# A projection stage that normalises and transposes its own input

## The chip, the cores and the metric

The kernel runs on one core of one Trainium2 chip. A core has a matrix engine (TensorE, PE in the profile; PEld is its weight load), a vector engine (VectorE, DVE), a scalar engine (ScalarE, ACT), a general one (GpSimd, POOL) and a synchronisation engine (SyncE, SP) that here only issues DMAs. The queue of DMAs that SyncE issues is q1, that of ScalarE q10. Each engine runs its own instructions in their order and meets the others at semaphores. The metric is the device time of one execution in microseconds; lower is better.

## The reference

The model has two layers on 8 sequences of 1024 tokens, 256 wide, all in float32. Only its first step matters here:

```python
def _layernorm(x, axis=-1, eps=1e-05):
    m = jnp.mean(x, axis=axis, keepdims=True)
    v = jnp.var(x, axis=axis, keepdims=True)
    return (x - m) / jnp.sqrt(v + eps)
...
def proj(W, b):
    return (x @ W + b).reshape(B, T, NUM_HEADS, HEAD_DIM).transpose(0, 2, 1, 3)
q = _rope(proj(Wq, bq))
k = _rope(proj(Wk, bk))
v = proj(Wv, bv)
```

Here `x` is the layer-normalised input. `_rope` multiplies two halves of each head by cosines and sines of the position and adds or subtracts them. Softmax attention over 16 heads, an output projection with a residual, a routed expert layer, a phase-memory attention and a soft mixture of experts follow; none of them is touched.

## The kernel before

The kernel is a row of stages. Each is a `Stage` with its own SBUF and PSUM buffers; at each start GpSimd raises every semaphore of the stage by one and all engines meet at a barrier, so that nothing of a stage overlaps the one before it. What passes between stages lies in DRAM.

Stage `n0` (`normalise`, lines 84 to 226) reads the 8 sequences, 1024 rows at a time. VectorE takes the statistics (`bn_stats` L149, `bn_aggr` L154), ScalarE the square root (L199), VectorE the reciprocal and minus mean over deviation (L166, L167) and the normalised rows (L175); TensorE transposes them, 16 tiles of 128x128 per sequence (L191), ScalarE copies them out of PSUM (L217) and stores the transposed array `xnT` (L222). For this stage no untransposed normalised rows are stored. The same function also serves two later stages, `n1` and `n3`.

Stage `qkv` (`qkv_rope`, from L229) takes 512 tokens at a time, 16 blocks. SyncE loads a block of `xnT` (L269) into one of four buffers. TensorE makes 128x512 products for the queries (two, each over two halves of the width: 4 matmuls), the same for the keys, both at L311, and 8 matmuls of 256 columns for the values (L318). A float32 matmul stands in the trace as two records of MATMUL, so a block has 16 of the first kind and 16 of the second. VectorE multiplies each product by the cosines and by the sines (L332, L333: four operations per unit, a unit being the queries or the keys of a block), GpSimd subtracts and adds (L350, L351, two operations per unit), VectorE adds the bias to the values (L340), and ScalarE issues the stores (L289, L293). Each engine's order is written out by hand. The products have two PSUM buffers, the values two as well.

In the code, `FLOOR` is the one by which each semaphore was raised; `made`, `multiplied`, `turned_ready`, `v_made` and `v_ready` count units or blocks that were finished by TensorE, VectorE, GpSimd, TensorE and VectorE.

## Time and profile before

| | |
|---|---|
| Median of 3 runs | 5393.15 us (5390.27 to 5396.76) |
| Span of the profiled execution, its own time | 5387.6 us |
| TensorE busy | 4725.5 us, 88% |
| VectorE busy | 3304.6 us, 61% |
| ScalarE busy | 2124.8 us, 39% |
| GpSimd busy | 1122.3 us, 21% |
| First instruction of the `qkv` stage's TensorE | 88.97 us after the span's start |
| First DMA of the attention stage | 266.82 us |

The profile is one execution; its span runs from the first to the last instruction, and its time is given by this span alone. The median of the timed runs is 5.6 us above it: that is what lies around the span, with the spread of the runs. In timelines a row is a run of like instructions: its start, how long it lasted together, engine, line, operation, output and inputs with buffer numbers left out, shapes and count; a bracket at the end is the engine's idle time before it and what ended that.

### The profile page before, as it was taken

The numbers are of one execution on the slowest core, as the hardware profiler recorded it, in microseconds if no ns is written. First come the engines' busy times: TensorE is split into PE (matmuls) and PEld (weight loads), VectorE is DVE, ScalarE is ACT, GpSimd is POOL, SyncE is SP. The second block draws the span as 40 slices with busy tenths as digits, with TensorE's granted clock in tenths as the row PEclk, the third lists the DMA queues.
The fourth block names the chain that finished last, engine by engine and source line by source line (L and its number), as shares of the span: only waits on it lengthen the run. The fifth ranks groups of instructions, "written<-read, shape, count | busy, mean of one in ns | idle before, by whom it ended". The sixth has DMA issues, their size and how long they took to land. (4 is left out here: it accounts for less than half of the span.)

```text
span 5387.6 us, 72176 instructions
## 1 busy us (share of the span) xinstructions
PE 4725.5 (88%) x28132; PEld 3108.0 (58%) x28132; DVE 3304.6 (61%) x3937; ACT 2124.8 (39%) x3450; POOL 1122.3 (21%) x848
## 2 busy tenths in 40 slices
PE   5879999999999755599997778774999999979999
PEld 3512222222222144488886334434899999968888
DVE  5578888888888344322222687775677676644443
ACT  1037777776677501122222434332222222223332
POOL 1432112222211020244442000000233333310000
PEclk9979999999999875799998889886999999989999
DMA  6543454443444184443433101109645444455543
GB/s 215 184 68 56 62 86 78 66 78 67 76 70 70 46 309 147 130 81 81 86 79 91 59 24 47 47 26 316 136 100 99 99 99 98 97 157 181 175 177 129
DMA packets 470402, 578.35 MB, mean 107 GB/s; under 512 B 32032, under 2 KB 384672, under 8 KB 461728
## 3 DMA queue, kind: packets, MB, share of 16 engines
q1 hardware_dynamic: 262816, 399.15, 28.6%
q10 hardware_dynamic: 182784, 142.62, 11.2%
q0 software_dynamic: 24576, 33.57, 3.8%
q8 instruction: 141, 2.31, 0.2%
q14 instruction: 85, 0.70, 0.1%
HBM read 297.23 MB, written 227.67 MB: 97 GB/s over the span
## 5 line engine op out<-in xcount | busy, mean ns | idle before, releaser
L743 DVE TENSOR_REDUCE att_nmx<-att_s 128x1 f32<-128x1024 f32 x1024 | 1204.9, 1219 | 230.9 <-PE att_s L653 227.6
L729 ACT ACTIVATE att_pt<-att_sT 128x512 f32<-128x512 f32 x2048 | 1058.9, 603 | 470.2 <-PE att_sT L670 469.6
L653 PE MATMUL att_s<-att_KT,att_QT 96*128 96x512 bf16 x2048 | 790.1, 390 | 48.1 <-DMA att_KT<-att_hi 38.0
L670 PE MATMUL att_sT<-att_QT,att_KT 128*128 128x512 bf16 x2048 | 778.2, 383 | 6.1 <-ACT att_pt L729 6.1
L1895 POOL TENSOR_TENSOR sl_lg<-sl_lg,sl_sm 128x512 f32<-128x512 f32 x256 | 319.5, 1269 | 1498.6 <-DVE sl_sm L2033 1498.6
L670 PEld LDWEIGHTS att_sT<-att_QT,att_KT 128*128 128x128 bf16 x2048 | 197.6, 97 | 650.1 <-ACT att_pt L729 466.9
L684 PE MATMUL att_o<-att_pt,att_va 128*32 128x512 f32 x4096 | 553.4, 607 | 0.0
L1906 PE MATMUL sl_lp<-sl_phi,sl_xT 128*128 (+1 forms) x4160 | 491.0, 277 | 36.5 <-DMA sl_xT<-xnT 22.8
L1906 PEld LDWEIGHTS sl_lp<-sl_phi,sl_xT 128*128 128x128 f32 x4160 | 478.4, 193 | 43.5 <-issue 43.5
L2146 PE MATMUL cb_op<-cb_y,cb_exT 128*128 128x256 f32 x2048 | 485.5, 380 | 0.0
L1944 PE MATMUL sl_acc<-sl_lg,sl_xn 128*128 128x128 f32 x4096 | 478.3, 275 | 0.0
L1944 PEld LDWEIGHTS sl_acc<-sl_lg,sl_xn 128*128 128x128 f32 x4096 | 467.7, 192 | 0.0
L1966 ACT ACTIVATE sl_lg<-sl_lg 128x1024 f32<-128x1024 f32 x128 | 135.3, 1057 | 767.2 <-DVE sl_lg L2022 767.2
L1356 DVE TENSOR_TENSOR moe_hT<-moe_sg,moe_up 128x512 f32<-128x512 f32 x128 | 88.1, 688 | 532.8 <-PE moe_yp L1221 325.4
L2146 PEld LDWEIGHTS cb_op<-cb_y,cb_exT 128*128 128x128 f32 x2048 | 370.7, 191 | 40.2
L653 PEld LDWEIGHTS att_s<-att_KT,att_QT 96*128 96x128 bf16 x2048 | 198.5, 99 | 244.7 <-DVE att_nmx L743 50.1
L2031 DVE TENSOR_REDUCE sl_sm<-sl_lg 128x128 f32<-128x1024 f32 x128 | 248.6, 1942 | 136.5 <-ACT sl_lg L1966 136.5
L1154 POOL DMA_INDIRECT x<-moe_y,moe_idx x128 | 213.2, 1666 | 344.2 <-ACT moe_y L1272 324.6
L579 POOL COPY att_QT<-att_QT 32x1024 bf16<-32x1024 bf16 x64 | 72.5, 1159 | 921.1 <-DVE att_QT L764 920.9
L1207 PE MATMUL moe_gp<-moe_xT,moe_wg 128*128 128x256 f32 x1024 | 244.0, 381 | 1.7 <-DVE moe_bo L1374 0.9
L1207 PE MATMUL moe_up<-moe_xT,moe_wu 128*128 128x256 f32 x1024 | 242.4, 380 | 0.0
L1221 PE MATMUL moe_yp<-moe_wd,moe_hT 128*128 128x256 f32 x1024 | 231.6, 379 | 1.4 <-DVE moe_hT L1356 1.4
(217 smaller groups left out, 6075.3 us busy)
## 6 DMA issues: line engine op xcount, KB each, us to landing
lg<-sl_raw ACTq DMA_DIRECT2D x128, 512.0 KB, 6.0
cb_ex<-lg SPq DMA_DIRECT2D x64, 1024.0 KB, 5.9
xnT<-n_xnT ACTq DMA_DIRECT2D x48, 512.0 KB, 5.5
n_x<-x SPq DMA_DIRECT2D x18, 1024.0 KB, 10.2
sl_w<-in_L_ffn_W SPq DMA_DIRECT2D x68, 256.0 KB, 3.5
qk<-qkv_turned ACTq DMA_DIRECT2D x64, 256.0 KB, 3.2
att_qin<-qk SPq DMA_DIRECT2D x64, 256.0 KB, 9.1
xn<-n_xn ACTq DMA_DIRECT2D x16, 1024.0 KB, 9.6
```

Of the source, the lines that this page charges most:

```text
L653: ins = pe.matmul(s[i % 2][:, c, :], QT[n % NB][0:ROWS, h, t * P:(t + 1) * P], KT[n % NB][0:ROWS, h, c * 512:(c + 1) * 512], start=True, s ...
L670: pe.matmul(sT[:, idx % 3, :], KT[g % NB][:, h, kt * P:(kt + 1) * P], QT[g % NB][:, h, step // 4 * 512:(step // 4 + 1) * 512], start=True, ...
L684: ins = pe.matmul(o[32 * h:32 * h + 32, :], va[g % 2][:, kt, h, :], pt[:, step % 2, h, c, :], start=kt == 0, stop=kt == NT - 1)
L729: act.activation(pt[:, step % 2, h, c, :], sT[:, idx % 3, :], ACT.Exp, scale=HD ** -0.5).then_inc(exp_done, 1)
L743: dve.tensor_reduce(nmx[n % 2][:, t, h:h + 1], s[i % 2][:].rearrange("p c k -> p (c k)"), AX.X, ALU.max, negate=True).then_inc(freed, 1)
L1207: ins = pe.matmul(o_[:, m, :], w_[:, k, (2 * h + m) * P:(2 * h + m + 1) * P], xT[n % 2][:, k, :], start=k == 0, stop=k == KD - 1)
L1221: ins = pe.matmul(yp[n % 2][:, s, :], hT[m // 2][:, m % 2, s * P:(s + 1) * P], wd[e][:, m, :], start=m == 0, stop=m == NI - 1)
L1895: pool.tensor_tensor(part_, part_, sm[j][:].rearrange("p (a n) -> p a n", a=1).broadcast_to([P, HB, P]), ALU.mult).then_inc(shared, 1)
L1906: ins = pe.matmul(lp[j][:, b, :], xT[:, k, b * T + m * P:b * T + (m + 1) * P], ph[:, k, bass.ds(c * P, P)], start=k == 0, stop=k == KD - 1)
L1944: ins = pe.matmul(acc[:, k, b, :], xn[:, b * NT + m, k * P:(k + 1) * P], lg[m % 4][:, b, :], start=m == 0 and b % 4 == 0, stop=m == NT - 1 ...
L2031: ch.link(dve.tensor_reduce(sm[j][:], lg[l][:].rearrange("p b n -> p n b"), AX.X, ALU.add))
L2146: ins = pe.matmul(op[n % 2][:], exT[n % 2][:, s, :], y[b % 2][:, s, :], start=s == 0, stop=s == SK - 1)
```

## The change

The separate stage `n0` is gone. `qkv_rope` now loads raw rows, 512 tokens at a time, into four buffers `xr` and does for each block what `n0` did: statistics (4 tiles of 256 elements), square root, reciprocal and scaled mean on VectorE and ScalarE. The normalised rows `xn` are now made by ScalarE (four operations with scale and bias per block) instead of VectorE. TensorE transposes 8 tiles of 128x128 into one PSUM buffer `tr`, and ScalarE takes all 1024 elements per partition out at once into `xT`. `xT` has two buffers instead of four, and the PSUM buffer of the values one instead of two. All stores of the stage are issued by SyncE instead of ScalarE, in one order with the loads: queries, next block's rows, keys, values.

```diff
-def qkv_rope(nc, xnT_d, wqk_d, ...
+def qkv_rope(nc, x_d, wqk_d, bqk_d, wv_d, bv_d, cos_d, sin_d, ident_d, qk_d, v_d):
...
+        xr = [st.sb(f"xr{j}", [P, TB, D]) for j in range(NR)]
+        xn = [st.sb(f"xn{j}", [P, TB, D]) for j in range(2)]
+        xT = [st.sb(f"xT{j}", [P, KD, N]) for j in range(2)]
-        vm = [st.ps(f"vm{j}", [P, N // P, D]) for j in range(2)]
+        vm = st.ps("vm", [P, TB, D])
+        tr = st.ps("tr", [P, KD, N])
...
             def _(sp):
                 def tokens(i):
-                    if i >= NX:
-                        sp.wait_ge(v_made, FLOOR + i - NX + 1)
-                    sp.dma_start(xT[i % NX][:], xnT_d[:, :, i * N:(i + 1) * N].rearrange("k p t -> p k t")
-                                 ).then_inc(x_in[i % NX], 16)
+                    if i >= NR:
+                        sp.wait_ge(xn_ready, FLOOR + i - NR + 1)
+                    sp.dma_start(xr[i % NR][:], rows(x_d, i)).then_inc(x_in[i % NR], 16)
...
                 tokens(0)
+                sp.dma_start(ident[:], ident_d).then_inc(ident_in, 16)
+                tokens(1)
                 sp.dma_start(wqk[:], wqk_d.rearrange("(k p) c n -> p k c n", p=P)).then_inc(c_in, 16)
...
+                tokens(2)
+                tokens(3)
+                for i in range(BLOCKS):
+                    unit_out(2 * i)
+                    if i + NR < BLOCKS:
+                        tokens(i + NR)
+                    unit_out(2 * i + 1)
+                    sp.wait_ge(v_ready, FLOOR + i + 1)
+                    sp.dma_start(rows(v_d, i), v[i % NV][:]).then_inc(v_stored[i % NV], 16)
...
             @block.tensor
+                def turn(i):
+                    pe.wait_ge(xn_ready, FLOOR + i + 1)
+                    if i >= 1:
+                        pe.wait_ge(xT_ready, FLOOR + i)
+                    for k in range(KD):
+                        for t in range(TB):
+                            ins = pe.transpose(tr[:, k, t * P:(t + 1) * P], xn[i % 2][:, t, k * P:(k + 1) * P], ident[:])
+                    ins.then_inc(across, 1)
...
+                pe.wait_ge(ident_in, FLOOR + 16)
+                turn(0)
+                pe.wait_ge(c_in, FLOOR + 16 * 6)
+                for i in range(BLOCKS):
+                    pe.wait_ge(xT_ready, FLOOR + i + 1)
+                    queries_or_keys(i, 0)
+                    if i + 1 < BLOCKS:
+                        turn(i + 1)
+                    queries_or_keys(i, 1)
+                    values(i)
...
             @block.scalar
+                def normal(i):
+                    act.wait_ge(nmr_ready, FLOOR + i + 1)
+                    if i >= 2:
+                        act.wait_ge(across, FLOOR + i - 1)
+                    for t in range(TB):
+                        ins = act.activation(xn[i % 2][:, t, :], xr[i % NR][:, t, :], ACT.Identity,
+                                             bias=nmr[i % 2][:, t:t + 1], scale=rstd[i % 2][:, t:t + 1])
+                    ins.then_inc(xn_ready, 1)
+                def take_turned(i):
+                    act.wait_ge(across, FLOOR + i + 1)
+                    if i >= 2:
+                        act.wait_ge(v_made, FLOOR + i - 1)
+                    act.activation(xT[i % 2][:], tr[:], ACT.Copy).then_inc(xT_ready, 1)
...
+                deviation(0)
+                normal(0)
+                deviation(1)
+                take_turned(0)
+                normal(1)
                 for i in range(BLOCKS):
+                    if i + 1 < BLOCKS:
+                        take_turned(i + 1)
+                    if i + 2 < BLOCKS:
+                        deviation(i + 2)
+                        normal(i + 2)
...
             @block.vector
+                for i in range(BLOCKS):
+                    rotate(2 * i)
+                    if i + 2 < BLOCKS:
+                        statistics(i + 2)
+                    rotate(2 * i + 1)
+                    if i + 2 < BLOCKS:
+                        scales(i + 2)
+                    dve.wait_ge(v_made, FLOOR + i + 1)
...
-    normalise(nc, "n0", x0, None, xnT, ident)
-    qkv_rope(nc, xnT, a["wqk"], ...
+    qkv_rope(nc, x0, a["wqk"], ... ident, qk, v)
```

`rotate` holds the four multiplications of a unit as they stood; `statistics` the `bn_stats` and `bn_aggr`; `scales` the reciprocal of `rstd`, then `nmr` from `mv` and `rstd`; `deviation` the square root. All four names take the place of lines that stood in `normalise` or `qkv_rope`.

On TensorE, a block before (the first; `mm` are the products of queries and keys, `vm` the values, x4 and x8 count matmuls):

```order
L311 MATMUL qkv_mm0<-qkv_xT0,qkv_wqk 128x512 x4
L311 MATMUL qkv_mm1<-qkv_xT0,qkv_wqk 128x512 x4
L318 MATMUL qkv_vm0<-qkv_wv,qkv_xT0 128x256 x8
L311 MATMUL qkv_mm0<-qkv_xT1,qkv_wqk 128x512 x4
L311 MATMUL qkv_mm1<-qkv_xT1,qkv_wqk 128x512 x4
```

And TensorE at the same place in the changed kernel, from the stage's first instruction on (`tr` is the transposes' PSUM buffer):

```order
L333 MATMUL qkv_tr<-qkv_ident,qkv_xn0 128x128 x8
L343 MATMUL qkv_mm0<-qkv_xT0,qkv_wqk 128x512 x4
L333 MATMUL qkv_tr<-qkv_ident,qkv_xn1 128x128 x8
L343 MATMUL qkv_mm1<-qkv_xT0,qkv_wqk 128x512 x4
L353 MATMUL qkv_vm<-qkv_wv,qkv_xT0 128x256 x8
L343 MATMUL qkv_mm0<-qkv_xT1,qkv_wqk 128x512 x4
L333 MATMUL qkv_tr<-qkv_ident,qkv_xn0 128x128 x8
L343 MATMUL qkv_mm1<-qkv_xT1,qkv_wqk 128x512 x4
```

The eight transposes of the next block stand between the queries and the keys of the present one.

VectorE in the first block before:

```order
L332 SCALAR_TENSOR_TENSOR qkv_by_cos0<-qkv_mm0,qkv_bqk,qkv_cos 128x512
L333 SCALAR_TENSOR_TENSOR qkv_by_sin0<-qkv_mm0,qkv_bqk,qkv_sin 128x512
L332 SCALAR_TENSOR_TENSOR qkv_by_cos1<-qkv_mm1,qkv_bqk,qkv_cos 128x512
L333 SCALAR_TENSOR_TENSOR qkv_by_sin1<-qkv_mm1,qkv_bqk,qkv_sin 128x512
L332 SCALAR_TENSOR_TENSOR qkv_by_cos1<-qkv_mm1,qkv_bqk,qkv_cos 128x512
L333 SCALAR_TENSOR_TENSOR qkv_by_sin1<-qkv_mm1,qkv_bqk,qkv_sin 128x512
L340 TENSOR_TENSOR qkv_v0<-qkv_vm0,qkv_bv 128x1024
```

VectorE in the first block of the changed kernel, from the end of the queries' unit on (`stats0`, `mv0`, `rstd0` and `nmr0` belong to the block after next):

```order
L436 SCALAR_TENSOR_TENSOR qkv_by_cos0<-qkv_mm0,qkv_bqk,qkv_cos 128x512
L437 SCALAR_TENSOR_TENSOR qkv_by_sin0<-qkv_mm0,qkv_bqk,qkv_sin 128x512
L411 BN_STATS qkv_stats0<-qkv_xr2 128x6 x4
L415 BN_AGGR qkv_mv0<-qkv_stats0 128x2 x4
L436 SCALAR_TENSOR_TENSOR qkv_by_cos1<-qkv_mm1,qkv_bqk,qkv_cos 128x512
L437 SCALAR_TENSOR_TENSOR qkv_by_sin1<-qkv_mm1,qkv_bqk,qkv_sin 128x512
L436 SCALAR_TENSOR_TENSOR qkv_by_cos1<-qkv_mm1,qkv_bqk,qkv_cos 128x512
L437 SCALAR_TENSOR_TENSOR qkv_by_sin1<-qkv_mm1,qkv_bqk,qkv_sin 128x512
L423 RECIPROCAL qkv_rstd0<-qkv_rstd0 128x4
L425 SCALAR_TENSOR_TENSOR qkv_nmr0<-qkv_mv0,qkv_rstd0 128x4
L456 TENSOR_TENSOR qkv_v0<-qkv_vm,qkv_bv 128x1024
```

The statistics stand between the two units, the reciprocal and `nmr` right behind the second unit and ahead of the values. `nmr` reads two tensors in SBUF.

## Rows read from the trace of the kernel before

**Rows 1.** The page's head.

```profile
span 5387.6 us, 72176 instructions
```

**Rows 2.** Windows: stretch, length, busy (count) by engine, clock, DMA share, GB/s.

```profile
0.00:78.00 78.00, 31.46 (x128) 25.10 (x128) 53.04 (x225) 21.36 (x42) 0.20 (x4) 1.00 0.66 230
78.00:89.00 11.00, 0.03 (x1) 0.03 (x1) 0.00 (x0) 0.00 (x0) 0.00 (x0) 1.00 0.91 277
89.00:256.00 167.00, 166.86 (x512) 97.81 (x512) 105.74 (x144) 0.00 (x0) 78.16 (x63) 1.00 0.60 186
```

**Rows 3.** Timeline, all engines, first stage: start us, length us, engine, line, operation.

```profile
2.41 0.45 SPq L128 DMA_DIRECT2D n_x<-in_x  x1
...
8.09 2.71 DVE L149 BATCH_NORM_STATS2 n_stats<-n_x 128x6 f32<-128x256 f32 x8 [5.55 <-DMA n_x<-in_x]
10.95 0.64 DVE L154 BATCH_NORM_AGGREGATE n_mv<-n_stats 128x2 f32<-128x6 f32 x8
...
12.97 0.30 ACT L199 ACTIVATE n_rstd<-n_mv,n_eps 128x8 f32<-128x8 f32 x1
...
15.04 0.17 DVE L166 RECIPROCAL n_rstd<-n_rstd 128x8 f32<-128x8 f32 x1
...
15.58 2.67 DVE L175 TENSOR_SCALAR n_xn<-n_x,n_rstd,n_nmr 128x256 f32<-128x256 f32 x8 [0.17 <-DVE n_nmr L167]
...
18.39 1.96 PE L191 MATMUL n_tr<-n_ident,n_xn 128*128 128x128 f32 x8 [18.39 <-DVE n_xn L175]
```

**Rows 4.** Timeline, all engines, between the first two stages.

```profile
77.96 0.37 SPq L269 DMA_DIRECT2D qkv_xT<-xnT  x1
...
88.97 8.63 PE L311 MATMUL qkv_mm<-qkv_xT,qkv_wqk 128*128 128x512 f32 x16 [18.69 <-DMA qkv_bv<-in_L_attn_bv]
```

**Rows 5.** Timeline, all engines, one block of the projection stage.

```profile
100.90 7.03 PE L311 MATMUL qkv_mm<-qkv_xT,qkv_wqk 128*128 128x512 f32 x16
...
104.53 0.75 DVE L332 SCALAR_TENSOR_TENSOR qkv_by_cos<-qkv_mm,qkv_bqk,qkv_cos 128x512 f32<-128x512 f32 x1 [2.21 <-PE qkv_mm L311]
...
107.34 1.27 POOL L350 TENSOR_TENSOR qkv_turned<-qkv_by_cos,qkv_by_sin 128x512 f32<-128x512 f32 x1 [4.39 <-DVE qkv_by_sin L333]
107.76 3.62 PE L318 MATMUL qkv_vm<-qkv_wv,qkv_xT 128*128 128x256 f32 x16
...
110.77 1.27 POOL L350 TENSOR_TENSOR qkv_turned<-qkv_by_cos,qkv_by_sin 128x512 f32<-128x512 f32 x1 [0.93 <-DVE qkv_by_sin L333]
...
111.22 7.03 PE L311 MATMUL qkv_mm<-qkv_xT,qkv_wqk 128*128 128x512 f32 x16
111.42 1.23 DVE L340 TENSOR_TENSOR qkv_v<-qkv_vm,qkv_bv 128x1024 f32<-128x1024 f32 x1 [0.72 <-PE qkv_vm L318]
```

**Rows 6.** Windows: a stretch of the second normalisation.

```profile
1990.00:2030.00 40.00, 21.82 (x89) 17.44 (x90) 34.34 (x148) 13.45 (x27) 0.00 (x0) 0.50 1.01 362
```

**Rows 7.** Timeline, TensorE, the same stretch.

```profile
1999.59 1.97 PE L191 MATMUL n_tr<-n_ident,n_xn 128*128 128x128 f32 x8 [1.21 <-ACT n_xnT L217]
```

**Rows 8.** Timeline, TensorE, last stage: transposes between matmuls.

```profile
5300.48 0.60 PE L2132 MATMUL cb_tr<-cb_ident,cb_ex 128*128 128x128 f32 x4
5300.92 1.89 PE L2146 MATMUL cb_op<-cb_y,cb_exT 128*128 128x256 f32 x8
```

**Rows 9.** Timeline, GpSimd and VectorE, in the attention stage.

```profile
1274.29 4.50 POOL L599 TENSOR_TENSOR att_num<-att_num,att_rb 128x2048 f32<-128x2048 f32 x1 [31.58 <-DMA att_num<-ctxT]
...
1274.33 4.51 DVE L754 CAST att_naug<-att_nrest 128x32 bf16<-128x32 f32 x1
```

**Rows 10.** Groups by line, ScalarE: count | busy us, mean ns | idle before.

```profile
L1970 ACT ACTIVATE sl_raw<-sl_lp 128x1024 f32<-128x1024 f32 x128 | 128.8, 1006 | 0.0
```

**Rows 11.** Timeline, ScalarE, scaled 256 elements, experts stage.

```profile
2506.22 0.84 ACT L1272 ACTIVATE moe_y<-moe_yp,moe_wt 128x256 f32<-128x256 f32 x2 [2.86 <-PE moe_yp L1221]
```

**Rows 12.** DMA view, 0 to 30 us: rate in 40 equal slices.

```profile
GB/s 0 0 0 0 26 83 296 382 384 348 339 355 351 347 347 350 345 347 350 350 350 320 23 0 0 22 147 284 384 386 175 0 0 0 53 61 232 429 396 384
```

**Rows 13.** The page, DMA issues: count, KB each, us to landing.

```profile
qk<-qkv_turned ACTq DMA_DIRECT2D x64, 256.0 KB, 3.2
```

More of the change, by code:

```diff
@@ L243, in qkv_rope @@
         sin = st.sb("sin", [P, T])
-        xT = [st.sb(f"xT{j}", [P, KD, N]) for j in range(NX)]
+        eps = st.sb("eps", [P, 1])
+        xr = [st.sb(f"xr{j}", [P, TB, D]) for j in range(NR)]
+        stats = [st.sb(f"stats{j}", [P, TB, 6]) for j in range(2)]
+        mv = [st.sb(f"mv{j}", [P, TB, 2]) for j in range(2)]
+        rstd = [st.sb(f"rstd{j}", [P, TB]) for j in range(2)]
+        nmr = [st.sb(f"nmr{j}", [P, TB]) for j in range(2)]
+        xn = [st.sb(f"xn{j}", [P, TB, D]) for j in range(2)]
+        xT = [st.sb(f"xT{j}", [P, KD, N]) for j in range(2)]
         by_cos = [st.sb(f"by_cos{j}", [P, 2, N]) for j in range(2)]
@@ L260, in qkv_rope @@
         table = lambda tab, u: tab[:, u // 2 % HALVES * N:(u // 2 % HALVES + 1) * N]
+        rows = lambda d, i: d[i * N:(i + 1) * N, :].rearrange("(t p) d -> p t d", p=P)
         with st.block() as block:
@@ L278, in _ @@
                 sp.dma_start(bv[:], col_bcast(bv_d)).then_inc(c_in, 16)
-                for i in range(1, BLOCKS):
-                    tokens(i)
+                tokens(2)
[7 more added lines that the diff above has]
+                    sp.dma_start(rows(v_d, i), v[i % NV][:]).then_inc(v_stored[i % NV], 16)
@@ new lines, in _, with queries_or_keys, values @@
+                for j in range(NO):
+                    sp.wait_ge(stored[j], FLOOR + 32 * (UNITS // NO))
+                for j in range(NV):
+                    sp.wait_ge(v_stored[j], FLOOR + 16 * len(range(j, BLOCKS, NV)))
+            @block.tensor
+            def _(pe):
+                def turn(i):
[6 more added lines that the diff above has]
+                    ins.then_inc(across, 1)
+                def queries_or_keys(i, w):
+                    u = 2 * i + w
+                    if u >= 2:
+                        pe.wait_ge(multiplied, FLOOR + u - 1)
+                    for two in range(2):
+                        for k in range(KD):
+                            ins = pe.matmul(mm[w][:, two, :], wqk[:, k, 2 * w + two, :], xT[i % 2][:, k, :],
+                                            start=k == 0, stop=k == KD - 1)
+                    ins.then_inc(made, 1)
+                def values(i):
+                    if i >= 1:
+                        pe.wait_ge(v_ready, FLOOR + i)
+                    for t in range(TB):
+                        for k in range(KD):
+                            ins = pe.matmul(vm[:, t, :], xT[i % 2][:, k, t * P:(t + 1) * P], wv[:, k, :],
+                                            start=k == 0, stop=k == KD - 1)
+                    ins.then_inc(v_made, 1)
+                pe.wait_ge(ident_in, FLOOR + 16)
[8 more added lines that the diff above has]
+                    values(i)
@@ L322, in _, with statistics @@
             @block.vector
             def _(dve):
-                dve.wait_ge(c_in, FLOOR + 16 * 6)
-                for u in range(UNITS):
+                def statistics(i):
+                    dve.wait_ge(x_in[i % NR], FLOOR + 16 * (i // NR + 1))
+                    for t in range(TB):
+                        ins = dve.bn_stats(stats[i % 2][:, t, :], xr[i % NR][:, t, :])
+                    ins.then_inc(stats_ready, 1)
+                    dve.wait_ge(stats_ready, FLOOR + i + 1)
+                    for t in range(TB):
+                        ins = dve.bn_aggr(mv[i % 2][:, t, :], stats[i % 2][:, t, :])
+                    ins.then_inc(var_ready, 1)
@@ new lines, in scales @@
+                def scales(i):
+                    dve.wait_ge(dev_ready, FLOOR + i + 1)
+                    if i >= 2:
+                        dve.wait_ge(xn_ready, FLOOR + i - 1)
+                    dve.reciprocal(rstd[i % 2][:], rstd[i % 2][:]).then_inc(rstd_ready, 1)
+                    dve.wait_ge(rstd_ready, FLOOR + i + 1)
+                    dve.scalar_tensor_tensor(nmr[i % 2][:], mv[i % 2][:, :, 0], -1.0, rstd[i % 2][:], ALU.mult, ALU.mult
+                                             ).then_inc(nmr_ready, 1)
```

84 lines of the change are left out of this document (38 added, 46 removed).

## The prediction

> **What bounds the kernel now.** I read first the page's head [rows 1] and its table of slices, to see that TensorE is the busiest engine nearly everywhere but at the start and in the gaps between stages; then the windows of the first 267 us, because the page's chain of waits is followed back from the end and says nothing of the start. In the windows [rows 2] the reader should see three kinds of stretch. From 0 to 78 us, the first normalisation, TensorE is busy 31.46 of 78 us and VectorE 53.04. From 78 to 89 us no engine works at all: the barrier is passed and the projection waits for its constants. From 89 to 256 us TensorE is busy 166.86 of 167 us and VectorE only 105.74, GpSimd 78.16, ScalarE 0: the projection stage is bound by TensorE. The timeline of a block [rows 5] shows the same in small: the matmuls of queries and keys start at 100.90, those of the values at 107.76, the next block's at 111.22, without a gap, a period of 10.32 us (16 records of 0.43 and 16 of 0.215). VectorE starts a unit 0.2 us behind its four matmuls (100.90 + 8 x 0.43 = 104.33, and 104.53) and waits 2.21 us for it. So work for ScalarE is free here, work for VectorE is free up to some 4 us a block, and work for TensorE is paid in full.
>
> **The change part by part.** The sum is made against the profiled execution's span, 5387.6 us; the timed median lies 5.6 us above it, and I carry that over.
>
> What goes: everything before the first matmul at 88.97 us [rows 4]. What comes instead is a new start, and then transposes inside a stage that TensorE bounds.
>
> The new start has two paths, and the later one decides. Both begin at SyncE's first DMA, at 2.41 us before [rows 3]. The stage now raises 28 semaphores instead of the 18 of the first normalisation; those 18 and the barrier took less than 2.0 us, so ten more cost between 0 and 1.1 us. I take 0.6: first DMA at 3.0.
> - Rows path. One megabyte landed 8.09 - 2.41 = 5.7 us after its issue. Half of it, at the 350 GB/s of [rows 12], lands 1.5 us sooner: 7.2. From the start of the statistics to the end of the square root it took 8.09 to 13.27 = 5.2 us with the loading of the function table; four tiles instead of eight take off half of 2.71 and half of 0.64, so 3.5: 10.7. Reciprocal and `nmr` take 15.58 - 15.04 = 0.54: 11.3. The normalised rows are new on ScalarE; the nearest row is a scaled operation of 256 elements, two in 0.84 [rows 11], so four in 1.6: 12.9 (VectorE needed 2.67 for eight, 1.3 for four, so either end is near). Eight transposes 1.96 [rows 3] and a handover of 0.1: 15.0. One copy of 1024 elements out of PSUM, 1.0 [rows 10], with 0.2 for the handovers: 16.2.
> - Constants path. Before, from the first DMA of the stage to the first matmul took 88.97 - 77.96 = 11.0 us [rows 4]. Now the identity and a second block of rows, 0.58 MB, stand ahead of the constants, 1.7 us at 350 GB/s: 3.0 + 12.7 = 15.7.
>
> So the first matmul of queries stands at 16.2 instead of 88.97: 72.8 us saved. Bounds: 14.5 if the semaphores cost nothing and the handovers are shorter, 18.5 if the two paths disturb one another. The slow start of TensorE is paid in both kernels: its first 16 records took 8.63 instead of 7.03 [rows 4, 5].
>
> Transposes: eight a block. The row of the first stage, eight in 1.96, seems to say 0.22 each. But the same operation takes the same time, 1.97, in the second normalisation [rows 7], where the granted clock is 0.50 [rows 6], that is the level of 1.2 GHz; so I read the clock of 1.00 shown for the first 78 us as not measured, and 0.22 as the slow level's price. In the last stage, where transposes stand between float32 matmuls at 1.00 (2.4 GHz), four take 5300.92 - 5300.48 = 0.44, or 0.11 each [rows 8]. The projection stage keeps TensorE busy without a gap, so its transposes should be of that kind: 8 x 0.11 = 0.87 us a block, a period of 10.32 + 0.87 = 11.19. The first block's transposes are in the start; 15 are left: 13.1 us added. Bounds: 0.87 and 1.76 a block.
>
> What lies beside TensorE. Take as zero the end of a block's query matmuls. VectorE begins at 0.2 and hands over to GpSimd 2.81 later (104.53 to 107.34 [rows 5]): 3.0. Four `bn_stats`, a gap and four `bn_aggr` take 1.36 + 0.15 + 0.32 = 1.8: 4.8. The key matmuls were done at 0.87 + 3.43 = 4.3, so VectorE begins them 0.3 us late, at 4.8, and ends at 7.6. Reciprocal and `nmr`: 8.2. ScalarE's four: 9.9. The transposes that want these rows stand one period on, at 11.19. Slack 1.3 us, so nothing. This is the wait that the change adds on TensorE, and behind it in its order stand the keys and the values: were it late, all of them would be, and VectorE with them. VectorE's work in a block is 2 x 2.81 + 1.8 + 0.54 + 1.23 = 9.2 of 11.19, ScalarE's 1.0 + 0.3 + 1.6 = 2.9. The single PSUM buffer of the values is read by VectorE within some 1.5 us after the last value matmul, and is wanted again 3.43 + 0.87 + 3.43 us later; the single one of the transposes is copied out in 1.2 us and wanted a block later. Nothing.
>
> The two operands of `nmr`. A small VectorE operation beside a running GpSimd one can be held: a cast of 128x32 took 4.51 us and ended with GpSimd's operation of 4.50 [rows 9]. Others run beside GpSimd unhindered: the addition to the values keeps its 1.23 though GpSimd started at 110.77, and GpSimd starts each unit about 0.1 us behind VectorE's last operation [rows 5], exactly where `nmr` now stands. If `nmr` waits for one GpSimd operation of 1.27 us, it is ready at 9.1 and the rows at 10.8: slack 0.4, still nothing. I take that. The Trainium skill ("SBUF — State Buffer", section "Who interferes with whom") says that VectorE and GpSimd share a pair of ports as an exclusive lock, and that a VectorE operation with two inputs in SBUF is fully blocked by a GpSimd one that reads SBUF. By that rule `nmr` is held in each block, where without it nothing would be; the trace agrees on the blocking, with 4.51 us, and by either reading the sum stays.
>
> Queue. All 2 MB a block now go through SyncE's queue: five issues besides the load, behind waits for GpSimd and VectorE. A block's rows are asked for two blocks before their statistics, 22 us, against landing times of 3 to 8 us. At 11.19 us a block that is 187 GB/s; this queue alone gave 350 in the first 20 us [rows 12]. Nothing. The stage's end has the same operations as before, so the tail to the attention stage is unchanged.
>
> Sum: -72.8 + 13.1 = -59.7 us. Span 5327.9, timed median **5333.5 us**.
>
> **The rivals.**
> - *Held twice.* GpSimd's two operations of a unit follow one another without a gap; if `nmr` gets through only behind both, it is ready at 10.3 and the rows at 12.0, 0.8 late. The chain reaches over two blocks, so a block pays half, 0.4: 14 x 0.4 = 5.6, 5339 us. For it: nothing shows who is let in first between two GpSimd operations. Against: after the cast of [rows 9] VectorE went on at once.
> - *Transposes at the slow price.* 15 x (1.76 - 0.87) = 13.3 more, 5347 us. For it: the only rows of this operation in this form, [rows 3, 7]. Against: the clock.
> - *`bn_stats` held too.* If the statistics also wait for both GpSimd operations (2.5 us), VectorE's block is 2.81 + 2.5 + 1.8 + 2.81 + 1.5 + 1.23 with 0.2 for a wait = 12.9 us and becomes the bound: 15 x 1.7 = 26, 5359 us. No row shows `bn_stats` beside GpSimd; the unhindered addition of [rows 5] speaks against.
> - *The one queue goes one transfer at a time.* Four stores of 3.2 us [rows 13] and two transfers twice their size, at least 3.2 each: 19.2 us a block instead of 11.19, 15 x 8.0 = 120 more, 5453 us, slower than before. It decides from a period of 11.19 + 59.7/16 = 14.9 us on. Against it: [rows 12], where the transfers of that queue overlapped, else 350 GB/s could not stand beside 5.7 us for one megabyte. The Trainium skill ("DMA: Bandwidth & Descriptors", section "Issuing engines are not separate DMA queues") has the queues of SyncE and ScalarE run on the same 16 engines, which would make the move free; no run here shows it yet.
>
> **How the numbers follow.** Forecast 0.66, held twice 0.13, slow transposes 0.08, `bn_stats` held 0.07, serial queue 0.03, and 0.03 for something larger that none of these names. The range: down by the start's lower bound (1.7) and the spread of the runs (3.6), 5328; up over held twice and the slow transposes with some of the start's upper bound, 5349. About 0.13 is left out. A change within 0.2%, 10.8 us, is what a measurement of this kernel cannot tell from none. All cases but the serial queue and part of the unnamed are faster by more: faster 0.95, same 0.01, slower 0.04.
>
> **What would show it.** In the changed profile: first matmul of queries near 16 us; TensorE's block every 11.2 us, with eight transposes taking 0.9 (1.8 would be the slow price) and no wait on them; `nmr` 0.2 or 1.3 or 2.5 us long; `bn_stats` four in 1.4, not 3.9; first DMA of the attention stage near 266.8 - 59.7 = 207. The forecast is wrong if TensorE waits for the normalised rows, or if the first matmul stands beyond 20 us.

## The result and the profile after

The changed kernel takes 5324.59 us (median of 4 runs, 5319.97 to 5327.42) against 5391.71 us for the kernel before (4 runs, 5387.21 to 5396.76) on the same chip: a ratio of 0.9877, 95% interval 0.9863 to 0.9891. The forecast was 5333.5 us with a range of 5328 to 5349. The gain was larger than forecast, and the time lies 3.4 us below the range. Two repetitions later gave 5322.05 and 5323.04 us, with ratios of 0.9877 and 0.9876.

The page of the profile after begins:

```profile
span 5323.5 us, 71820 instructions
```

That answers to [rows 1], 64.1 us less. This execution's own time was 5325.72 us, so 2.2 us lie around the span.

The windows of the first 208 us, in the columns of [rows 2]:

```profile
0.00:16.30 16.30, 1.94 (x8) 1.57 (x8) 4.22 (x21) 4.95 (x9) 0.20 (x4) 1.00 0.70 244
16.30:195.00 178.70, 178.64 (x625) 109.11 (x626) 143.82 (x282) 50.43 (x89) 77.07 (x62) 1.00 0.56 169
195.00:208.00 13.00, 1.86 (x9) 1.30 (x7) 2.40 (x3) 0.09 (x1) 2.81 (x3) 0.74 0.39 121
```

The reader should see that the 89 us ahead of the first matmul have become 16.3, and that in the whole stage behind it TensorE is busy 178.64 of 178.70 us: it never waits for the rows that VectorE and ScalarE now make.

The start, timeline of all engines, in the columns of [rows 3]:

```profile
3.19 0.46 SPq L290 DMA_DIRECT2D qkv_xr<-in_x  x1
...
7.06 1.40 DVE L411 BATCH_NORM_STATS2 qkv_stats<-qkv_xr 128x6 f32<-128x256 f32 x4 [3.74 <-DMA qkv_xr<-in_x]
8.50 0.38 DVE L415 BATCH_NORM_AGGREGATE qkv_mv<-qkv_stats 128x2 f32<-128x6 f32 x4
8.96 1.28 ACT L373 ACT_TABLE_LOAD   x1 [8.96 <-DVE qkv_mv L415]
10.26 0.30 ACT L373 ACTIVATE qkv_rstd<-qkv_mv,qkv_eps 128x4 f32<-128x4 f32 x1
...
10.80 0.16 DVE L425 SCALAR_TENSOR_TENSOR qkv_nmr<-qkv_mv,qkv_rstd 128x4 f32<-128x4 f32 x1
...
13.21 1.94 PE L333 MATMUL qkv_tr<-qkv_ident,qkv_xn 128*128 128x128 f32 x8 [13.21 <-ACT qkv_xn L381]
...
16.36 5.68 PE L343 MATMUL qkv_mm<-qkv_xT,qkv_wqk 128*128 128x512 f32 x8 [1.20 <-ACT qkv_xT L390]
```

The chain is the forecast one: rows, statistics, square root behind the loading of its table, normalised rows, transposes, copy out of PSUM, first matmul at 16.36 us where 16.2 was worked out. The bracket of the last row says that it waited for the copy. The last of the constants, the values' bias, had been issued at 7.20 and landed 8.2 us later, at 15.4 (forecast for that path: 15.7), so the two paths end within a microsecond of each other.

One block, timeline of all engines, answering to [rows 5]:

```profile
100.24 1.04 PE L333 MATMUL qkv_tr<-qkv_ident,qkv_xn 128*128 128x128 f32 x8
...
101.12 3.60 PE L343 MATMUL qkv_mm<-qkv_xT,qkv_wqk 128*128 128x512 f32 x8
...
103.09 1.40 DVE L411 BATCH_NORM_STATS2 qkv_stats<-qkv_xr 128x6 f32<-128x256 f32 x4
103.25 1.27 POOL L466 TENSOR_TENSOR qkv_turned<-qkv_by_cos,qkv_by_sin 128x512 f32<-128x512 f32 x1 [4.36 <-DVE qkv_by_sin L437]
...
104.55 3.62 PE L353 MATMUL qkv_vm<-qkv_wv,qkv_xT 128*128 128x256 f32 x16
...
107.59 1.26 POOL L466 TENSOR_TENSOR qkv_turned<-qkv_by_cos,qkv_by_sin 128x512 f32<-128x512 f32 x1 [1.85 <-DVE qkv_by_sin L437]
107.63 1.24 DVE L425 SCALAR_TENSOR_TENSOR qkv_nmr<-qkv_mv,qkv_rstd 128x4 f32<-128x4 f32 x1
...
108.00 3.60 PE L343 MATMUL qkv_mm<-qkv_xT,qkv_wqk 128*128 128x512 f32 x8
...
108.80 1.21 DVE L456 TENSOR_TENSOR qkv_v<-qkv_vm,qkv_bv 128x1024 f32<-128x1024 f32 x1
108.81 1.27 POOL L467 TENSOR_TENSOR qkv_turned<-qkv_by_sin,qkv_by_cos 128x512 f32<-128x512 f32 x1
...
108.91 2.08 ACT L381 ACTIVATE qkv_xn<-qkv_xr,qkv_nmr,qkv_rstd 128x256 f32<-128x256 f32 x4 [3.67 <-DVE qkv_nmr L425]
...
111.44 1.04 PE L333 MATMUL qkv_tr<-qkv_ident,qkv_xn 128*128 128x128 f32 x8
```

From one set of transposes to the next it is 11.20 us (forecast 11.19); eight transposes stand 0.88 ahead of the next matmul (forecast 0.87). `nmr` is four numbers per partition wide and lasts 1.24 us: it ends with the GpSimd operation that started 0.04 before it, and GpSimd's next one, which starts at 108.81, does not hold it again. The statistics run in 1.40 us beside GpSimd, as fast as alone (1.40 at 7.06). The rows are ready at 108.91 + 2.08 = 110.99, and the transposes that read them stand at 111.44: 0.45 us are left, where 0.4 was expected.

The waits of PEld from 20 to 195 us (us in total, times, longest) show how near that is:

```profile
PEld qkv_tr L333 <- ACT qkv_xn L381: 3.7, 14, 0.4
```

The weight load, which runs ahead of the matmuls, has to wait a little in each of 14 blocks; for the matmuls themselves there is no such row.

The attention stage's first DMA stands at 207.91 us where it was at 266.82: 58.9 us earlier (forecast 59.7, at 207). The span is shorter by 64.1. So 5.2 us came from behind the stage, where nothing was edited.

### The profile page after: what moved, and what is told of

It reads as the page before. It is cut to its first block and busy times, and to the rows that moved or that the text cites. A ratio compares the mean times of both kernels' runs of the same rounds, so it can differ in the third digit from the quotient of the medians.

```text
span 5323.5 us, 71820 instructions
## 1 busy us (share of the span) xinstructions
PE 4691.7 (88%) x27974; PEld 3096.4 (58%) x28132; DVE 3293.2 (62%) x3873; ACT 2158.1 (41%) x3505; POOL 1122.1 (21%) x848
## 5 line engine op out<-in xcount | busy, mean ns | idle before, releaser
L786 PE MATMUL att_sT<-att_QT,att_KT 128*128 128x512 bf16 x1890 | 718.6, 383 | 6.8 <-ACT att_pt L845 6.7
## 6 DMA issues: line engine op xcount, KB each, us to landing
n_x<-x SPq DMA_DIRECT2D x18, 1024.0 KB, 10.8
```

Source lines behind the costliest of these rows:

```text
L786: pe.matmul(sT[:, idx % 3, :], KT[g % NB][:, h, kt * P:(kt + 1) * P], QT[g % NB][:, h, step // 4 * 512:(step // 4 + 1) * 512], start=True, ...
```

## The experiments

Each kernel was timed beside the kernel before on the same chip. Its median there was 5388.96 us (29 runs) for e1 to e4, 5388.57 (11 runs) for e5 to e8 and 5389.13 (13 runs) for e9 to e12.

### e1 and e2: both kernels again

No edit. What was expected of the changed kernel:

> The changed kernel again, unchanged. The stage itself came out as worked out (attention's first DMA at 207.9 us, 58.9 earlier than before), but from there to the end the profiled execution took 5115.6 us against 5120.8 before. Theory spread: those 5.2 us are the spread of single executions; the ratio comes nearer to 0.989 (59 us), and the rest behind 207.9 us lies anywhere from 5112 to 5122 us. Rival lasting gain: the later stages gain something in every execution; ratio 0.9875 again (67 us) and the rest again 5115 to 5117 us.

And of the kernel before:

> The kernel before again, against itself. Theory spread: ratio 1.000 within 0.001, and the rest of the span behind the attention's first DMA differs from the 5120.8 us of the first profile by some us. Rival lasting gain: the rest is 5120 to 5122 us again.

The changed kernel took 5322.05 us (4 runs, ratio 0.9877, 0.9863 to 0.9892), span 5318.4; the kernel before 5388.55 (11 runs, ratio 0.9999, 0.999 to 1.0007), span 5381.6 in an execution of 5383.48. The changed kernel's ratio came again, as the lasting gain foresaw it; the spread foresaw 0.989. But the part behind attention's first DMA was 5109.4 and 5114.7 us in these two profiles, 6 us below the first profile of either kernel, so a single profile does not give its size. Two of the numbers that the forecast started from also look different: the median of 3 runs lay 4 us above that of 29, and what lies around a span is 2 us (1.9 here, 2.2 after), not the 5.6 that came from setting the median against one execution's span.

### e3: the removed stage put back, its output unread

```diff
+    normalise(nc, "n0", x0, None, xnT, ident)
     qkv_rope(nc, x0, a["wqk"], ...
```

> The changed kernel with the separate first normalisation left in front of it, its output read by nobody, so that only the fusion's price is left: transposes inside the stage, new start. The stage before took 266.8 - 78.0 = 188.8 us from its first DMA to the attention's, the changed one 207.9 - 3.2 = 204.7. Both theories: the attention's first DMA at 78 + 205 = 283 us, 16 later than before. Theory spread: total 16 us above before, 5408 (ratio 1.0030). Rival lasting gain through what left with the first stage (its traffic, its 8 MB written): also 16 us. Rival lasting gain through something in the new stage: only 8 to 11 us above before.

5400.2 us (11 runs, ratio 1.0023, 1.0014 to 1.0032), slower than before; attention's first DMA at 283.6 us against 208 to 209 in the changed kernel. Its TensorE at the start of the projection, in the columns of the timelines:

```profile
88.38 1.94 PE L333 MATMUL qkv_tr<-qkv_ident,qkv_xn 128*128 128x128 f32 x8 [18.05 <-ACT qkv_xn L381]
91.53 5.89 PE L343 MATMUL qkv_mm<-qkv_xT,qkv_wqk 128*128 128x512 f32 x8 [1.21 <-ACT qkv_xT L390]
97.26 1.04 PE L333 MATMUL qkv_tr<-qkv_ident,qkv_xn 128*128 128x128 f32 x8
```

This separates the two terms. The stage n0 costs 283.6 - 208.5 = 75.1 us and is what is saved; the work taken into the projection costs 283.6 - 266.9 = 16.7 us against the kernel before, of which 15 x 0.88 = 13.2 are transposes, and 2.5 the first matmul's coming at 91.5 instead of 89.0. Of the last 1.0, 0.7 is a slower start: the first eight records took 5.89 us, 2.3 more than the 3.60 of later ones, where the kernel before lost 1.6 (8.63 against 7.03). Since the total is only 11.2 us above before, its later stages too are some 5 us shorter. Of the three forecasts that of a lasting gain in the new stage (8 to 11 us above before) is the nearest, though the interval, 7.5 to 17.2 us above before, just takes in the 16 of the other two.

### e4 and e5: the stores' queue by itself

e4 is the kernel before with the projection's stores on SyncE (its loads and stores in the changed kernel's order); e5 is the changed kernel with the stores back on ScalarE.

```diff
-                    act.wait_ge(turned_ready, FLOOR + u + 1)
+                    sp.wait_ge(turned_ready, FLOOR + u + 1)
                     for two in range(2):
-                        act.dma_start(qk_d[b, w, :, two * 8:two * 8 + 8, t0:t0 + N], ...
+                        sp.dma_start(qk_d[b, w, :, two * 8:two * 8 + 8, t0:t0 + N], ...
```

> The kernel before with one part of the change alone: the projection stage's stores are issued by SyncE in one order with its loads. If one queue carries all without loss: the same time, ratio 1.000 within 0.001, block period 10.32 us. Rival serial queue: 19 us a block, 140 us more, ratio 1.026. Rival lasting gain from the stores' queue: ratio 0.9985, 8 us less.

> The changed kernel with one part undone: the stage's stores are issued by ScalarE again, in its order between the copies and the normalised rows. ScalarE then has 2.9 us of work and some 3 us of issuing in a block of 11.2. Stage: if nothing waits, attention's first DMA at 208 to 209 us as before this edit; if the waits in front of the stores hold back the normalised rows, up to 1 us more a block. Behind that point: theory queue (what the later stages gain, 6 us by the medians, comes from keeping these stores off ScalarE's queue): the rest returns to about 5120 us, total 5328. Rival spread between programs (each program has its own few us, unrelated to the queue): the rest stays near 5114, total 5322.

e4 took 5384.57 us (12 runs, ratio 0.9994, 0.9985 to 1.0003), attention's first DMA at 266.3; e5 5327.16 (4 runs, 0.9884, 0.9869 to 0.9899), that DMA at 208.5. Neither differs from its base within the intervals. The serial queue is refuted: with everything on one queue the kernel before keeps its block of 10.32 us, and e5, with two queues, has the changed kernel's 11.20:

```profile
100.37 7.03 PE L313 MATMUL qkv_mm<-qkv_xT,qkv_wqk 128*128 128x512 f32 x16
107.23 3.62 PE L320 MATMUL qkv_vm<-qkv_wv,qkv_xT 128*128 128x256 f32 x16
110.69 7.03 PE L313 MATMUL qkv_mm<-qkv_xT,qkv_wqk 128*128 128x512 f32 x16
```

By the rule of the Trainium skill that was weighed ("DMA: Bandwidth & Descriptors", section "Issuing engines are not separate DMA queues"), that DMAs run on the same 16 DMA engines whichever engine issues them, the move should be free; the two periods agree.

Whether the queue has a part in what the later stages gained is not settled by these two. e4's interval reaches down to 0.9985, just what the rival foresaw, and its median lies 4.4 us below before. e5's median of 5327.2 is nearer to the queue's 5328 than to 5322, but its profile has 5112.4 us behind attention's first DMA, not 5120, and e7 below, with all stores on SyncE, has a median of 5326.4 too.

### e6: every transpose done twice

```diff
-                    for k in range(KD):
+                    for k in range(2 * KD):
+                        k = k % KD
                         for t in range(TB):
```

> The changed kernel with every transpose made twice. Theory: a transpose between float32 matmuls at the full clock costs TensorE 0.11 us, so 8 more a block cost 15 x 0.87 = 13 us, and 1.7 to 2 us more once at the start: 15 us, total 5337. Rival slow price (0.22 each): 15 x 1.76 + 2 = 28, total 5350. Rival hidden (TensorE not the bound): 2 us.

5337.8 us (4 runs, ratio 0.9897, 0.9883 to 0.9911), period 12.07 us: 0.87 more for eight more transposes, so TensorE pays them in full at 0.11 each; taken off the 11.20 of the changed kernel, the same 0.87 leaves the old period. That the total hit the forecast 5337 is partly luck: attention's first DMA stands at 220.3 us, 12.4 later than the 207.9 of the changed kernel and not 15, and the attention stage behind it came out 5 us longer in the profile. TensorE's start and a later set, timeline:

```profile
13.16 3.32 PE L334 MATMUL qkv_tr<-qkv_ident,qkv_xn 128*128 128x128 f32 x16 [13.16 <-ACT qkv_xn L382]
17.69 3.67 PE L344 MATMUL qkv_mm<-qkv_xT,qkv_wqk 128*128 128x512 f32 x8 [1.21 <-ACT qkv_xT L391]
21.20 1.91 PE L334 MATMUL qkv_tr<-qkv_ident,qkv_xn 128*128 128x128 f32 x16
```

The first matmuls take 3.67 here and 5.68 in the changed kernel, which is where the start's share of the forecast went. What TensorE had done before them differs: 3.32 us of transposes here and 1.94 there, with 1.2 us of idle time behind either.

### e7: `nmr` moved out of GpSimd's way

VectorE makes the reciprocal and `nmr` ahead of the keys' products instead of behind them.

```diff
                         statistics(i + 2)
-                    rotate(2 * i + 1)
-                    if i + 2 < BLOCKS:
                         scales(i + 2)
+                    rotate(2 * i + 1)
```

> The changed kernel with the reciprocal and nmr of a block moved ahead of the keys' unit on VectorE. Theory: nmr is held there too, but the rows are ready some 3 us earlier and TensorE does not wait for them in either order; VectorE has 2 us to spare; time unchanged within 2 us (5322), block period 11.20. Rival (the hold of 1.24 us costs something today): faster, up to 0.25 us a block, 4 us. Rival (VectorE becomes late with the keys' unit and holds TensorE): slower by 1 us a block, 5337.

5326.38 us (4 runs, ratio 0.988, 0.9866 to 0.9895): no change. `nmr` takes 0.29 us instead of 1.24, in the timeline

```profile
105.14 1.26 POOL L466 TENSOR_TENSOR qkv_turned<-qkv_by_sin,qkv_by_cos 128x512 f32<-128x512 f32 x1
...
106.13 0.29 DVE L425 SCALAR_TENSOR_TENSOR qkv_nmr<-qkv_mv,qkv_rstd 128x4 f32<-128x4 f32 x1
```

(the first row is GpSimd's), and the period stays 11.20. `nmr` is held here too, but only for the rest of a GpSimd operation that began 1 us before it: both end at 106.4. The hold costs nothing, as forecast: it lay in slack.

### e8: the normalised rows 2 us later

ScalarE makes them twice, first into a buffer that nobody reads.

```diff
+                    if i >= 2:
+                        for t in range(TB):
+                            act.activation(spare[:, i, t, :], xr[i % NR][:, t, :], ACT.Identity,
+                                           bias=nmr[i % 2][:, t:t + 1], scale=rstd[i % 2][:, t:t + 1])
                     for t in range(TB):
```

> The changed kernel in which ScalarE makes the four normalised tiles of a block twice, first into a buffer nobody reads: the rows are ready 4 x 0.5 = 2.0 us later. They were ready 0.25 us before TensorE could take them, so they come 1.75 late. Theory: the chain from one block's queries to the transposes of the block after next spans two periods, so a block pays half, 0.9 us, 14 x 0.9 = 12 us, total 5334, block period 12.1. Rival full price: 14 x 1.75 = 25 us, total 5347, period 12.95. Rival nothing (slack larger than read): 5322.

5348.68 us (6 runs, ratio 0.9917, 0.9904 to 0.993). Timeline of TensorE and ScalarE:

```profile
111.18 1.09 PE L334 MATMUL qkv_tr<-qkv_ident,qkv_xn 128*128 128x128 f32 x8 [1.38 <-ACT qkv_xn L386]
...
119.87 2.08 ACT L383 ACTIVATE qkv_spare<-qkv_xr,qkv_nmr,qkv_rstd 128x256 f32<-128x256 f32 x4 [5.24 <-DVE qkv_nmr L430]
...
121.85 2.07 ACT L386 ACTIVATE qkv_xn<-qkv_xr,qkv_nmr,qkv_rstd 128x256 f32<-128x256 f32 x4
...
123.97 1.09 PE L334 MATMUL qkv_tr<-qkv_ident,qkv_xn 128*128 128x128 f32 x8 [1.38 <-ACT qkv_xn L386]
```

The period is 12.79, 1.59 more, and attention's first DMA stands at 230.0, 22.1 us later: the rival's full price, and not half of it. A delay of 2.07 that costs 1.59 leaves a slack of 0.48, which is the 0.45 seen between the rows and the transposes in the changed kernel. The rows of block i+2 hang on `nmr`, this on the keys' products of block i, and those on the keys' matmuls of block i, which stand behind the transposes of block i+1. So the loop from one set of transposes to the next closes within one period.

### e9, e10 and e12: what changed behind the stage

Comparing the profiles stage by stage, the shorter later part lies in two places: the attention stage (1631.8 and 1629.2 us from its first DMA to the output projection in the kernel before; 1628.1, 1626.5 and 1627.5 in the changed one) and the soft slots. The stretch between these two places scatters by 10 us over all runs (1831.8 to 1841.7) and is on average equal in the two kernels; it is where single executions differ most. In the attention GpSimd multiplies `num` by `rb`, one instruction of 4.5 us [rows 9], eight times, and small VectorE operations beside it are held. Groups of VectorE in the attention stage, before (columns of [rows 10]):

```profile
L768 DVE COPY att_QT<-att_QT 32x1024 bf16<-32x1024 bf16 x32 | 23.1, 723 | 5.0 <-DVE att_QT L764 0.5
L754 DVE CAST att_naug<-att_nrest 128x32 bf16<-128x32 f32 x32 | 10.8, 338 | 1.1
L753 DVE TENSOR_TENSOR att_nrest<-att_nmx,att_naug 128x32 f32<-128x32 f32 x32 | 10.4, 324 | 1.1
```

and after:

```profile
L884 DVE COPY att_QT<-att_QT 32x1024 bf16<-32x1024 bf16 x32 | 25.5, 798 | 4.6
L871 DVE TENSOR_TENSOR att_naug<-att_nrest,att_naug 128x32 bf16<-128x32 f32 x32 | 11.5, 359 | 1.1
L870 DVE CAST att_naug<-att_nrest 128x32 bf16<-128x32 f32 x32 | 6.5, 204 | 1.1
L869 DVE TENSOR_TENSOR att_nrest<-att_nmx,att_naug 128x32 f32<-128x32 f32 x32 | 6.2, 193 | 1.1
```

Two such holds of some 4.3 us before, one after: the cast L754 took 10.8 us against 6.5 after (L870), the subtraction L753 10.4 against 6.2 (L869), and after it is L871 that is dearer, 11.5 against 7.3 before (L755). The repeated profile before again has two, the two repeated ones after again one. But the copy `att_QT` can be held for the length of the multiply as well, and after it is the dearer (25.5 against 23.1); VectorE beside one of the multiplies, which starts at 1217.76 in the changed kernel:

```profile
1218.73 3.85 DVE L884 COPY att_QT<-att_QT 32x1024 bf16<-32x1024 bf16 x1
```

So the instruction was cut up, in the kernel before (e9) and in the changed one (e10), and the changed one was run once more beside them (e12):

```diff
-                    pool.tensor_tensor(num[:], num[:], rb[:], ALU.mult).then_inc(divided, 1)
+                    for k in range(KD):
+                        for q in range(NT):
+                            c = slice(q * P, (q + 1) * P)
+                            ins = pool.tensor_tensor(num[:, k, c], num[:, k, c], rb[:, k, c], ALU.mult)
+                    ins.then_inc(divided, 1)
```

> The kernel before, with GpSimd's multiply num*rb of the attention (one instruction of 4.5 us on 4 x 512 columns) cut into 16 instructions of 128 columns. Theory (the later stages came out shorter in the changed kernel because one small VectorE operation fewer is held for the length of that multiply): no small VectorE operation of the attention lasts over 1 us beside it any more, both holds of 4.3 us are gone, the wait of the matmuls of scores on att_nmx falls from 35.6 to under 31 us, and the stretch from attention's first DMA to the projection from 1631.8 to 1620 to 1625. The time falls by 4 to 9 us, to about 5382. Rival (the shorter later stages have another cause): the stretch stays at 1629 to 1633 and the time within 2 us of before, or it grows, since 16 instructions cost GpSimd more than one.

> The changed kernel with the same edit, GpSimd's multiply num*rb in 16 pieces. Theory: the one hold of 4.3 us goes, the stretch from attention's first DMA to the projection falls from 1628 to the same 1620 to 1625 as in the kernel before with the pieces, and the difference between the two kernels with pieces shrinks from 65 to 59 to 62 us; time about 5320. Rival: the difference between the two stays at 65, the stretch stays shorter here by 3 to 4 us.

> The changed kernel once more, unchanged, as the base of the other three on this chip. 5322 to 5325, some 65 us below the kernel before; one VectorE operation of the attention held for 4.3 us, the stretch of the attention 1626 to 1629.

e9 took 5374.61 us (8 runs, ratio 0.9971, 0.996 to 0.9981), e10 5311.2 (4 runs, 0.9857, 0.9839 to 0.9875), e12 5323.04 (4 runs, 0.9876, 0.9859 to 0.9894). The held groups in e10, where L875 and L888 are L871 and L884 of the changed kernel:

```profile
L888 DVE COPY att_QT<-att_QT 32x1024 bf16<-32x1024 bf16 x32 | 16.5, 517 | 4.6
L875 DVE TENSOR_TENSOR att_naug<-att_nrest,att_naug 128x32 bf16<-128x32 f32 x32 | 7.5, 233 | 1.1
L874 DVE CAST att_naug<-att_nrest 128x32 bf16<-128x32 f32 x32 | 6.5, 203 | 1.1
L873 DVE TENSOR_TENSOR att_nrest<-att_nmx,att_naug 128x32 f32<-128x32 f32 x32 | 6.2, 192 | 1.1
```

The holds are gone. TensorE's wait for them (its matmuls of the scores, ended by `att_nmx`; us in total, times, longest) was, in the kernel before,

```profile
PE att_s L647 <- DVE att_nmx L743: 35.7, 31, 5.2
```

and is, in e9,

```profile
PE att_s L651 <- DVE att_nmx L747: 28.1, 31, 1.4
```

where the longest no longer has the length of a hold. In the changed kernel it falls from 31.2 to 27.1, and the attention stretch is 1617.9 us in e9 and 1618.4 in e10: equal, where it differed by about 3, and below the 1620 to 1625 expected. GpSimd's long multiply is thus what made the attention differ.

How it did so is less clear than the count of two holds and one suggests. With the copies counted, VectorE's operations were held for 13 to 14 us in either kernel (before 4.3 + 4.2 + 23.1 - 17.7 for the copies in e9; after 4.0 + 25.5 - 16.5), so the changed kernel has not less holding but holding of other operations. TensorE's other matmuls of the scores, those with `att_KT`, waited 7.6 us for `att_nmx` before and 9.8 after, so of the 4.5 us gained on one line 2.2 are lost on the other. Nor is the number of small operations held the change's merit: with e4, whose only edit is the queue, there were three holds and 1636.5 us, with e6 two and 1633.4. Why an edit ahead of the attention shifts which operation meets GpSimd's was not settled.

In the totals the pieces gave 14.5 us and 11.8 us, more than the 4 to 9 expected and near the 13 to 14 of everything held. The distance of the two kernels went from 66.1 to 63.4 us, not to 59 to 62; with intervals of 5 to 10 us to either side for each kernel against before, the totals do not decide it, and the theory rests on the stretches.

The other place is open. From the slots' first matmul to the last stage it took 1092.2, 1089.6, 1087.9 and 1092.1 us in the four kernels with the old stage (before, e2, e4, e9), and 1085.2 to 1089.2 in the ten with the new one. TensorE's wait for the loads of `xn` there is 13.7, 12.7, 10.1 and 13.7 us in the first four and at most 10.6 in the others. The two groups meet: e4 lies among the kernels with the new stage in both numbers. e9 keeps its 13.7, so GpSimd's multiply is not its cause. No experiment was aimed at it.

### e11: the start shortened

On top of e10: ScalarE takes a square root of constants first, so that the table is loaded early; the weights of queries and keys get a semaphore of their own; TensorE transposes the identity 20 times while it waits.

```diff
+                act.activation(early[:], eps[:], ACT.Sqrt, bias=eps[:, 0:1])
...
-                sp.dma_start(wqk[:], wqk_d.rearrange("(k p) c n -> p k c n", p=P)).then_inc(c_in, 16)
+                sp.dma_start(wqk[:], wqk_d.rearrange("(k p) c n -> p k c n", p=P)).then_inc(w_in, 16)
...
+                for _ in range(20):
+                    pe.transpose(tr[:, 0, 0:P], ident[:], ident[:])
...
-                pe.wait_ge(c_in, FLOOR + 16 * 6)
+                pe.wait_ge(w_in, FLOOR + 16)
...
+                    if i == 0:
+                        pe.wait_ge(c_in, FLOOR + 16 * 5)
```

> The changed kernel with the multiply in 16 pieces and a shorter start: ScalarE runs one Sqrt on a column of constants first, so that its table load of 1.28 us no longer stands between the statistics and the first square root; the weights of queries and keys have a semaphore of their own, and only the values of block 0 wait for the five other constants; TensorE transposes the identity 20 times while it waits for the first rows. Theory: the square root starts behind the aggregation at 8.9 instead of 10.26, the first matmul of queries at 15.0 instead of 16.36 and its eight last 3.6 instead of 5.68, so attention's first DMA comes near 204 instead of 207.9; time about 5316, some 4 below the one with the pieces alone. Rival: the first matmuls are late for their weights (the weight load of block 0 ended its wait at 16.33), then the start gains under 1 us.

5310.19 us (5 runs, ratio 0.985, 0.9835 to 0.9865), the fastest of all, but within the interval of e10. The start itself does what was expected:

```profile
7.39 4.53 PE L361 MATMUL qkv_tr<-qkv_ident 128*128 128x128 f32 x20 [7.39 <-DMA qkv_ident<-in_ident]
...
11.89 1.34 PE L335 MATMUL qkv_tr<-qkv_ident,qkv_xn 128*128 128x128 f32 x8
...
14.44 3.67 PE L345 MATMUL qkv_mm<-qkv_xT,qkv_wqk 128*128 128x512 f32 x8 [1.21 <-ACT qkv_xT L396]
```

First matmul at 14.44 instead of 16.36 and its set 2.0 us shorter; attention's first DMA comes at 203.9 instead of 208.0 in e10. The 4.1 us are seen in the trace, and not proved in the total, where the executions of one set differ by 7 to 21 us.

## Why the prediction was right and where it was wrong

**The stage itself: right.** The removed start (first matmul at 16.36, forecast 16.2), the transposes (11.20 a block, forecast 11.19), no wait on TensorE, `nmr` held by one GpSimd operation, unheld statistics and attention's first DMA (207.91, forecast 207) all came as worked out. e3 separates gain and price, e6 shows that the transposes are paid in full, e7 that the hold is free, e4 and e5 that the queue is, as far as the stage goes. Neither of the two signs of being wrong that were named appeared, a wait for the normalised rows or a late first matmul: nothing watched what lies behind the stage. Reading the clock of 1.00 in the first 78 us as not measured was right as well: the changed kernel's own transposes fall from 1.94 for eight at the start to 1.04 in the stream. As for the rule of the Trainium skill that was weighed ("SBUF — State Buffer", section "Who interferes with whom"), that the ports which the two engines share are an exclusive lock, for which a VectorE operation with two inputs in SBUF contends with a GpSimd one that reads SBUF, the trace agrees: `nmr`, with two SBUF inputs, waited for the GpSimd operation that had begun 0.04 us earlier; at the stage's start, with GpSimd idle, it took 0.16. The cast of [rows 9], which the prediction set beside this rule, reads one tensor only: it shows an operation blocked, but not this case of two inputs.

**The later stages: the step that failed.** The sum took everything behind the stage as unchanged, and had no term and no bound for it. Against the 59.7 forecast the gain was 67.1, 66.9 and 66.1 us in three sets of runs, and 61.4 and 62.2 in e5 and e7, whose stage is as long. The stage has 58 to 59 of it, so 3 to 8 us came from behind, 6 on average. In the profiles that part was 5120.8 and 5114.7 us in the kernel before and 5115.6, 5109.4 and 5109.8 in the changed one, 6 less on average. About 3 of that are in the attention and go away when GpSimd's multiply is cut up, as e9 and e10 show; about 3 lie in the slots stage and are unexplained, and a part of the stores' queue in them is not excluded. [Rows 9] had one hold of 4.51 us in it, and it was read for `nmr` alone, not as something that a shift of the order of events could remove or add. A term of plus or minus 4.3 us for one hold would have taken the range to 5324.

**The base: up to 4 us too high.** The step "the timed median lies 5.6 us above it, and I carry that over" took a median of 3 runs for a property of the kernel. A fourth run brought it from 5393.15 to 5391.71, and later sets of 29, 11 and 13 runs gave 5389. Whether the rest was chance in few runs or lay in that set is not shown: the changed kernel was 2 us slower there too (5324.59 against 5322.05 and 5323.04). The execution profiled before lay, with some 2 us around its span, at about 5389.6. From 5389.0 the same sum gives 5329.3, with the range 4 us lower as well. The measured time would then have been just inside it, by luck, with the same step wrong.

**The start of TensorE and the tail: 0.8 us short.** The stage gained 58.9 us and not 59.7. The first matmul was 0.2 later. "The slow start of TensorE is paid in both kernels" was mis-sized: it cost 8.63 - 7.03 = 1.6 us before and 5.68 - 3.60 = 2.1 in the changed kernel. The last 0.1 lies between the last matmuls and the next stage.

**ScalarE's term: mis-sized without effect.** The four scaled operations took 2.08 us, not the 1.6 taken from [rows 11], where the input was another. But `nmr` was ready 8.6 us after the queries' matmuls (108.87 - 100.24) where 9.1 was worked out, so the rows came at 10.75 against the 10.8 forecast.

**"So a block pays half": wrong.** In the rival "held twice" the delay was spread over two blocks. e8 shows a delay of 2.07 us costing 1.59 a block, all beyond the slack, so the loop closes in one period. By that, a second hold of 1.23 us would have cost about 0.75 us a block (an estimate: 1.23 less the slack of 0.48), and not 0.4.

## What to carry to other kernels

When a change is worked out stage by stage, give the untouched stages a term of their own: look for long GpSimd instructions beside VectorE's small ones, where a meeting can hold the small one for nearly the length of the long one, and put one of them more or fewer into the range. Take the base from many executions and not from three, and not from the profiled one either: the two profiled executions of the kernel before have spans of 5387.6 and 5381.6 us. Work out the gain apart from the base, so that an error in one does not hide one in the other. And if a GpSimd instruction of some us stands beside a chain of small VectorE operations that TensorE waits for, try it in pieces: 16 pieces took 14.5 us off the kernel before, though GpSimd itself works longer that way.

## What the runs showed of the hardware

- A small VectorE operation held by GpSimd gets through between two GpSimd operations that follow one another: `nmr` ended at 107.63 + 1.24 = 108.87 with the first, though the second followed at once, at 108.81. It is held for the rest of the operation that it meets: 1.24 us where that had begun 0.04 us earlier, 0.29 where it had begun 1 us earlier (e7).
- Four `bn_stats` on float32 rows take 1.40 us beside a GpSimd operation and without one. Scaled float32 operations of 256 elements on ScalarE with scale and bias from SBUF take 2.08 us for four.
- The same four 128x512 products (eight records) took 5.68 us behind 1.94 us of TensorE work with an idle time of 1.20, and 3.67 behind 3.32 us of it with an idle time of 1.21 (e6).
- GpSimd's multiply of 2048 columns takes 4.52 us; its pieces of 128 columns take about 0.42 each, one behind the other (ten in 4.18 us), so cutting costs GpSimd half as much again; the kernel before became 14.5 us shorter by it, the changed one 11.8.
